# Three of sixteen sequences of a shared expert moved into the head of the next stage, and scatters that read their places directly

## Chip, core and metric

The kernel runs on one core of one Trainium2 chip. The metric is the device time of one execution in microseconds; lower is better. It is the median of several executions.

## What is computed

Four layers follow each other on 16 sequences of 256 tokens with 256 features, all in float32. Each is added to its input behind a layer norm, of which the second layer, a mixture of experts with a shared expert for all tokens, and the third, a state space layer, matter here.

```python
def _swiglu(t, wa, wb, wo):
    h = jax.nn.silu(t @ wa.T) * (t @ wb.T)
    return h @ wo.T
# layer 0, feed forward: 16 experts of width 176, top 2; shared width 352
scores = jax.nn.softmax(t @ gate_w.T, axis=-1)
weights, indices = jax.lax.top_k(scores, TOP_K)
for e in range(N_EXPERTS):
    w_e = jnp.sum(jnp.where(indices == e, weights, 0.0), axis=-1)
    y = y + _swiglu(t, w1[e], w3[e], w2[e]) * w_e[:, None]
z = _swiglu(t, sw1, sw3, sw2)          # the shared expert, of every token
return y + z
...
x = x + _layernorm(_L0_attn_ref(_layernorm(x), ...))
x = x + _layernorm(_L0_ffn_ref(_layernorm(x), ...))
x = x + _layernorm(_L1_attn_ref(_layernorm(x), ...))   # state space layer
x = x + _layernorm(_L1_ffn_ref(_layernorm(x), ...))    # 16 experts, top 8
```

## The kernel before

Each engine has a program of its own, written in the order in which it runs; semaphores tie them together. No scheduler moves anything: what a generator of steps yields first comes first on every engine that has a part in it. A step names its work, and each engine's function for that stage picks its share. x stays in SBUF (32 tiles of 128 tokens, two for a sequence).

The kernel goes through three parts. The first is attention, to about 436 us. The second is `SparseMoe`, the first mixture of experts. The third is `Tail`, the fused loop of the state space layer and the second mixture of experts, from about 822 us.

`SparseMoe` has two stages. In the **shared stage** `shared_steps` yields, for each of 16 sequences, the steps of the shared expert: "norm" (VectorE writes the normed rows), "turn_x" (TensorE transposes them in 4 pieces, ScalarE copies them out of PSUM), three chunks "up" (8 multiplications each, then silu on ScalarE and the product with the other half on VectorE, L769), and "down" (12 multiplications, L559; ScalarE copies the result, SyncE stores it to `results`). The hidden width of 704 makes three chunks for silu and product, of 128, 128 and 96 rows. The down step of a sequence stands behind the first up chunk of the next. Among these steps stand the "choose" steps (VectorE finds the two experts of each token and its place in a list sorted by expert) and, from the fifth sequence on, one "scatter" behind each chunk, for the 32 tiles. In a scatter VectorE writes a tile's rows into one of two buffers `pairs` (L685, L779), after it has waited for the DMAs that last read that buffer; GpSimd copies the places (L818), does an addition that nobody reads (L819), and issues two indirect DMAs (L822), which write the rows to `sorted_in` in HBM. SyncE waits for all scatters before it fetches the first sorted rows (L863).

In the **routed stage** 80 blocks of 128 sorted rows are fetched and go through their experts (L528, L599, L610, L620).

In the **tail**, `Tail.head` yields the steps with which the loop begins. "c_fetch" loads the three results of each token of a sequence, "c_sum" and "c_norm" (L2074 to L2089) add them and write the new x; "norm", "turn_x" (L1689), "feat" (L1701), "bcdt" (L1708), "turn_dt" (L1714), "dt", "table", "turn_dA" (L1731), "gate" (L1723), "conv" and "silu" prepare the state space layer of sequence 0; "turn_c" (L1740) and "xdt" (L1933) end this. Then `period` yields 18 rows of steps for each sequence, a table `THEN` saying what stands in which. The first scan of the decays (L1942, L1945) and its weighting (L1951) open period 0. Table loads of ScalarE (ACT_TABLE_LOAD) come where the activation function changes its set.

In PSUM there are eight banks; in the tail banks 4 to 6 (`UP_BANK`) and 7 (`SUM_BANK`) belong to the second mixture of experts and are unused in the head.

## Time and profile before

| | |
|---|---|
| median of 3 runs | 1965.39 us (1960.80 to 1970.16) |
| the profiled execution, its own time | 1962.86 us |
| span of its profile | 1961.1 us |
| busy share of the span | TensorE 93%, VectorE 64%, ScalarE 39%, GpSimd 22% |
| mean granted clock of TensorE | 0.96 of full |
| chain that ended last, by engine | TensorE 45%, issue 38%, VectorE 9%, GpSimd 4% |
| shared stage | 436 to 587 us |
| routed stage | 587 to 820 us |
| head of the tail, to the first scan weighting | 822 to 871 us |

A timeline row reads: start in us, duration in us, engine, line, operation, what is written and from what, shapes, how many instructions are merged. In brackets stands the idle time of the engine before it and what ended that. PE is TensorE's multiplications, PEld its weight loads, DVE VectorE, ACT ScalarE, POOL GpSimd, SPq the DMA queue of SyncE. A row of windows reads: stretch, its length, busy time (and instructions) of PE, PEld, DVE, ACT and POOL, the granted clock as a share of 2.4 GHz, the DMA engines' busy share, GB/s. Busy shares tell little here, since the stages have different bounds; the waits in each stage are what counts.

### The profile page before, as it was taken

How to read it: one execution, taken by the hardware profiler on the slowest of the kernel's cores; microseconds unless marked ns; L12 is line 12 of the kernel's file. 1: busy time of each engine (PE TensorE's matmuls, PEld its weight loads, DVE VectorE, ACT ScalarE, POOL GpSimd, SP SyncE). 2: the span in 40 equal slices, each digit the busy share in tenths (PEclk: the TensorE clock that was granted, in tenths of full speed). 3: DMA queues.
4: the chain of work that ended last, by engine and by line, in shares of the span. 5: the costliest groups of instructions: out<-in, count | busy, mean ns of one | idle time of the engine just before them, and what ended most of it. 6: DMA issues, size and time to landing. Idle time of an engine off the chain costs nothing.

```text
span 1961.1 us, 33597 instructions
## 1 busy us (share of the span) xinstructions
PE 1831.5 (93%) x9969; PEld 1414.6 (72%) x9987; DVE 1264.7 (64%) x3621; ACT 763.2 (39%) x1479; POOL 422.5 (22%) x708
## 2 busy tenths in 40 slices
PE   5999999979989999667999999999999999999998
PEld 3566666547776666445888888888888888888886
DVE  3677677527432222368778877887787778777843
ACT  1466666543223333234433343334333333433321
POOL 1244334331763444300100110011001100110000
PEclk9899999879998999867999999999999999999999
DMA  9900000001332333252012202220222022112210
GB/s 359 220 6 1 0 0 1 1 1 38 114 108 84 94 94 93 81 199 81 25 63 87 82 16 76 87 81 6 87 85 63 25 86 81 46 46 71 66 49 11
DMA packets 92119, 137.87 MB, mean 70 GB/s; under 512 B 18548, under 2 KB 76148, under 8 KB 91508
## 3 DMA queue, kind: packets, MB, share of 16 engines
q1 hardware_dynamic: 85108, 117.83, 19.0%
q0 software_dynamic: 6912, 18.92, 2.7%
q8 instruction: 38, 0.62, 0.1%
q14 instruction: 61, 0.50, 0.1%
HBM read 98.51 MB, written 38.22 MB: 70 GB/s over the span
## 4 chain that ended last, share of the span: by engine, by line
PE 45%; issue 38%; DVE 9%; POOL 4%; ACT 2%; DMA 1%; another core or an unknown queue 1%; DVEq 0%; SPq 0%; POOLq 0%; ACTq 0%
PE bank L599 6%; PE bank L184 5%; PE bank L1151 4%; PE bank L620 4%; PE bank L1216 3%; PE bank L1109 2%; PE bank L548 2%; PE bank L193 2%; PE bank L1157 2%; PE bank L1244 2%; PE bank L1139 2%; PE bank L559 1%; PE bank L610 1%; PE bank L1202 1%; PE bank L528 1%
## 5 line engine op out<-in xcount | busy, mean ns | idle before, releaser
L184 PE MATMUL bank<-moe_xT,up_w 128*128 128x256 f32 x2304 | 546.1, 380 | 0.0
L184 PEld LDWEIGHTS bank<-moe_xT,up_w 128*128 128x128 f32 x2304 | 438.7, 191 | 60.0
L227 ACT ACTIVATE moe_silu<-bank 128x256 f32<-128x256 f32 x288 | 110.4, 383 | 575.6 <-PE bank L184 572.4
L193 PE MATMUL bank<-down_w,moe_hT 128*128 128x256 f32 x1152 | 304.0, 387 | 3.5 <-ACT moe_y L230 2.1
L193 PEld LDWEIGHTS bank<-down_w,moe_hT 128*128 128x128 f32 x1152 | 207.1, 190 | 37.0 <-issue 6.4
L1390 DVE TENSOR_REDUCE q_slots<-bank 128x4 f32<-128x1024 f32 (+1 forms) x96 | 117.7, 1226 | 82.2 <-PE bank L1151 81.6
L1298 ACT ACTIVATE probs<-bank 128x1024 f32<-128x1024 f32 x96 | 98.1, 1022 | 100.4 <-PE bank L1157 100.4
L599 PE MATMUL bank<-up_w,moe_xT 128*128 x320 | 116.8, 488 | 0.7 <-ACT moe_xT L663 0.6
L794 DVE TENSOR_TENSOR moe_h<-moe_silu,bank 128x176 f32<-128x176 f32 x80 | 27.0, 338 | 138.8 <-issue 86.4
L1151 PE MATMUL bank<-kT,qT 16*128 16x256 f32 (+1 forms) x1024 | 115.3, 353 | 0.2 <-issue 0.2
L294 DVE TENSOR_TENSOR moe_hT<-moe_silu,bank 128x256 f32<-128x256 f32 x256 | 107.7, 421 | 8.8
L1157 PE MATMUL bank<-qmT,kT 17*128 17x512 f32 x384 | 111.2, 652 | 1.3 <-ACT probs L1298 1.3
L293 DVE TENSOR_TENSOR moe_silu<-moe_silu,up_w 128x256 f32<-128x256 f32 x192 | 81.1, 423 | 46.5 <-ACT moe_silu L227 41.0
L326 POOL TENSOR_TENSOR moe_prstd<-moe_pmv,minus_half 128x2 f32<-128x2 f32 x16 | 12.2, 759 | 451.7 <-DVE moe_pmv L304 451.7
L1151 PEld LDWEIGHTS bank<-kT,qT 16*128 16x128 f32 x1024 | 79.5, 193 | 31.5 <-issue 28.5
L548 PE MATMUL bank<-moe_s_xT,up_w 128*128 128x256 f32 (+1 forms) x384 | 90.5, 385 | 4.8 <-ACT moe_s_xT L638 2.5
L620 PE MATMUL bank<-down_w,moe_hT 88*128 x320 | 84.7, 387 | 3.8 <-issue 3.2
L838 POOL DMA_INDIRECT results<-moe_result,moe_home x80 | 79.2, 990 | 20.2 <-POOL pool_spare L837 15.0
L1945 DVE TENSOR_TENSOR_SCAN m<-m,delta 128x256 f32<-128x256 f32 x128 | 81.5, 678 | 2.2
L548 PEld LDWEIGHTS bank<-moe_s_xT,up_w 128*128 128x128 f32 (+1 forms) x384 | 69.4, 184 | 18.5 <-ACT moe_s_xT L638 3.3
L1923 DVE SCALAR_TENSOR_TENSOR conv<-feat,taps,conv 128x256 f32<-128x256 f32 x192 | 80.1, 478 | 1.8 <-ACT conv_bc L1839 1.2
L599 PEld LDWEIGHTS bank<-up_w,moe_xT 128*128 128x128 f32 x320 | 55.2, 192 | 28.5 <-issue 9.3
(287 smaller groups left out, 3181.5 us busy)
## 6 DMA issues: line engine op xcount, KB each, us to landing
up_w<-comb_rows SPq DMA_DIRECT2D x32, 768.0 KB, 6.0
m<-decay_rows SPq DMA_DIRECT2D x16, 1024.0 KB, 4.9
comb_got<-results SPq DMA_DIRECT2D x16, 768.0 KB, 7.7
moe_rows<-sorted_in SPq DMA_DIRECT2D x80, 128.5 KB
sorted_in<-zero SPq DMA_DIRECT2D x10, 1024.0 KB, 9.5
down_w<-comb_rows SPq DMA_DIRECT2D x16, 512.0 KB, 8.4
up_w<-in_up SPq DMA_DIRECT2D x2, 3168.0 KB, 15.0
up_w<-in_up SPq DMA_DIRECT2D x2, 2304.0 KB, 11.9
```

The costliest lines, as they stand in the source:

```text
L184: last = mm(k.bank[:, UP_BANK + i % 3, half * S:(half + 1) * S], m.w_up[:, c, at + half * m.inter:at + (half + 1) * m.inter], m.xT[:, par, ...
L193: last = mm(k.bank[:, SUM_BANK, j * D:(j + 1) * D], m.hT[:, i % 3, j * P:(j + 1) * P], m.w_down[:, m.expert(i), :], start=(i == 0 and j == ...
L227: nc.scalar.activation(m.silu[:, i % 3, :], k.bank[:, UP_BANK + i % 3, 0:S], ACT.Silu).then_inc(m.silu_ready, 1)
L294: tt(m.hT[:, i % 3, :], m.silu[:, i % 3, :], u, ALU.mult).then_inc(m.h_ready, 1)
L548: last = nc.tensor.matmul(k.bank[0:w, 2 + c, half * S:(half + 1) * S], m.w_up[:, f, lo + half * 2 * inter:lo + half * 2 * inter + w], m.s_ ...
L599: last = nc.tensor.matmul(k.bank[:, 2 + par, 0:2 * inter], m.xT[:, par, c, :], cols(m.w_up[:, c, :], expert, 2 * inter), start=(c == 0), s ...
L620: last = nc.tensor.matmul(k.bank[:, 6 + par, 0:D], m.hT[0:m.half, par, c, :], w_down[0:m.half, bass.ds(expert * 2 * D + c * D, D)], start= ...
L1151: last = mm(k.bank[:, SCORE_BANK + lane, r * keys:(r + 1) * keys], m.qT[rows, its, qb, half * per + r, :], m.kT[rows, its, 0:keys], start= ...
L1157: last = mm(k.bank[:, PROB_BANK + lane, :], m.kT[rows, par, phalf * P:(phalf + 1) * P], m.qmT[rows, pqb].rearrange("p r n -> p (r n)"), st ...
L1298: activation(m.probs[:, (i + 2 * par) % 4].rearrange("p g r n -> p (g r n)"), k.bank[:, PROB_BANK:PROB_BANK + PAIR, :].rearrange("p b n -> ...
L1390: v.tensor_reduce(m.q[:, par, qb, half * per:(half + 1) * per, heads[0]:heads[0] + PAIR, HD].rearrange("p r g -> p g r"), k.bank[:, SCORE_ ...
L1945: last = v.tensor_tensor_scan(to[:, 0:S], to[:, 0:S], m.delta[:], 0.0, ALU.mult, ALU.add)
```

## The change

Two things change in the shared stage. It runs over 13 sequences (`EARLY`) instead of 16. The 32 scatters are spread over the 27 places behind the chunks of sequences 4 to 12; five places hold two. GpSimd reads a tile's places directly from `places`, without the copy and the addition. There are two buffers of rows (`PAIR_ROWS`), as before.

The last three sequences, a, b and c in `head`, are computed in the head of the tail by new steps: l_norm, l_turn, l_up (three), l_h (three), l_down and l_end. They use the buffers and PSUM banks of the second mixture of experts, single buffers except for xT. Their stores go through SyncE's queue, and l_end, behind period 0, waits for them.

```diff
+PAIR_ROWS = 2
+EARLY = 13
...
+    places = chunks * (EARLY - SCATTERS_FROM)
...
-    for t in range(B):
+    for t in range(EARLY):
...
-            if t >= SCATTERS_FROM and tile < TILES:
+            place = chunks * (t - SCATTERS_FROM) + c + 1
+            while place > 0 and tile < -(-TILES * place // places):
                 yield "scatter", tile, 0
                 tile += 1
...
-        self.place = sb("moe0_place", [P, 4], U32)
-        self.pairs = sb("moe0_pairs", [P, 2, 2, ROW])
+        self.pairs = sb("moe0_pairs", [P, PAIR_ROWS, 2, ROW])
...
-            par = t % 2
-            if begun(t - 1):
-                dve.wait_ge(m.scattered[par], (t - par) * 16)
+            row = t % PAIR_ROWS
+            if t >= PAIR_ROWS:
+                dve.wait_ge(m.scattered[row], 2 * 16 * (t // PAIR_ROWS))
             for j in range(2):
-                normalise(m.pairs[:, par, j, 0:D], t)
-            v.tensor_copy(m.pairs[:, par, :, D].bitcast(U32), cols(k.pair_no, t, 2)).then_inc(m.rows_ready, 1)
+                normalise(m.pairs[:, row, j, 0:D], t)
+            v.tensor_copy(m.pairs[:, row, :, D].bitcast(U32), cols(k.pair_no, t, 2)).then_inc(m.rows_ready, 1)
...
-            par = t % 2
+            row = t % PAIR_ROWS
             pool.wait_ge(m.rows_ready, t + 1)
-            chain.link(g.tensor_copy(m.place[:, 2 * par:2 * par + 2], cols(m.places, t, 2)))
-            g.tensor_tensor(k.pool_spare[:, 0:1], k.minus_half[:, 0:1], k.minus_half[:, 0:1], ALU.add)
             for j in range(2):
-                at = bass.IndirectOffsetOnAxis(m.place[:, 2 * par + j:2 * par + j + 1], 0)
-                g.indirect_dma_start(m.sorted_in, at, m.pairs[:, par, j, :], None).then_inc(m.scattered[par], 16)
+                at = bass.IndirectOffsetOnAxis(m.places[:, 2 * t + j:2 * t + j + 1], 0)
+                g.indirect_dma_start(m.sorted_in, at, m.pairs[:, row, j, :], None).then_inc(m.scattered[row], 16)
...
+    def step(what, t, par, c):
+        n = t - EARLY
+        if what == "l_turn":
+            pe.wait_ge(s.xn_ready, t + 1)
+            pe.wait_ge(s.y_read, t)
+            for f in range(KD):
+                for j in range(SEQ_TILES):
+                    last = nc.tensor.transpose(k.bank[:, SUM_BANK, (f * SEQ_TILES + j) * P:(f * SEQ_TILES + j + 1) * P],
+                                               moe.xn[:, j, f * P:(f + 1) * P], k.ident[:])
+            last.then_inc(s.xT_full, 1)
+        if what == "l_up":
+            w, lo = s.wide(c), E * 2 * s.inter + c * P
+            pe.wait_ge(s.xT_ready, m.turns + n + 1)
+            if n > 0:
+                pe.wait_ge(s.h_ready, m.up(t - 1, c) + 1)
+            for half in range(2):
+                for f in range(KD):
+                    last = nc.tensor.matmul(k.bank[0:w, UP_BANK + c, half * S:(half + 1) * S],
+                                            s.w_up[:, f, lo + half * 2 * s.inter:lo + half * 2 * s.inter + w],
+                                            moe.xT[:, t % 2, f, :], start=(f == 0), stop=(f == KD - 1))
+            last.then_inc(s.up_full, 1)
+        if what == "l_down":
+            pe.wait_ge(s.h_ready, m.up(t + 1, 0))
+            for j in range(SEQ_TILES):
+                for c in range(s.shared_chunks):
+                    w = s.wide(c)
+                    last = nc.tensor.matmul(k.bank[:, SUM_BANK, j * D:(j + 1) * D], moe.hT[0:w, c, j * P:(j + 1) * P],
+                                            s.w_down[0:w, 2 * E + c, :], start=(c == 0), stop=(c == s.shared_chunks - 1))
+            last.then_inc(s.y_full, 1)
+        if what == "l_end":
+            pe.wait_ge(s.y_read, B)
...
+        n = t - EARLY
+        if what == "l_turn":
+            act.wait_ge(s.xT_full, m.turns + n + 1)
+            nc.scalar.copy(moe.xT[:, t % 2].rearrange("p c t -> p (c t)"), k.bank[:, SUM_BANK, :]).then_inc(s.xT_ready, 1)
+        if what == "l_up":
+            w = s.wide(c)
+            act.wait_ge(s.up_full, m.up(t, c) + 1)
+            if n > 0:
+                act.wait_ge(s.h_ready, m.up(t - 1, c) + 1)
+            nc.scalar.activation(moe.silu[0:w, c, :], k.bank[0:w, UP_BANK + c, 0:S], ACT.Silu).then_inc(s.silu_ready, 1)
+        if what == "l_down":
+            act.wait_ge(s.y_full, m.turns + n + 1)
+            if n > 0:
+                act.wait_ge(s.stored[(t - 1) % 2], 16 * ((t - 1) // 2 + 1))
+            nc.scalar.copy(moe.y[:].rearrange("p j d -> p (j d)"), k.bank[:, SUM_BANK, :]).then_inc(s.y_read, 1)
+        if what == "l_end":
+            for stored in s.stored:
+                act.wait_ge(stored, 16 * B // 2)
...
+        n = t - EARLY
+        if what == "l_norm":
+            if n > 0:
+                dve.wait_ge(s.xT_full, m.turns + n)
+            for j in range(SEQ_TILES):
+                last = normalised(k, moe.xn[:, j, :], SEQ_TILES * t + j)
+            last.then_inc(s.xn_ready, 1)
+        if what == "l_h":
+            w = s.wide(c)
+            dve.wait_ge(s.silu_ready, m.up(t, c) + 1)
+            if n > 0:
+                dve.wait_ge(s.y_full, m.turns + n)
+            k.nc.vector.tensor_tensor(moe.hT[0:w, c, :], moe.silu[0:w, c, :], k.bank[0:w, UP_BANK + c, S:2 * S],
+                                      ALU.mult).then_inc(s.h_ready, 1)
...
+        if what == "l_down":
+            sp.wait_ge(s.y_read, t + 1)
+            sp.dma_start(s.shared_rows(t), moe.y[:]).then_inc(s.stored[t % 2], 16)
+        if what == "l_end":
+            for stored in s.stored:
+                sp.wait_ge(stored, 16 * B // 2)
...
-        for what, t, i in (("c_fetch", 0, 0), ("c_sum", 0, 0), ("c_sum", 0, 1), ("c_norm", 0, 0), ("c_fetch", 1, 0),
-                           ("experts", 0, 0)):
+        a, b, c = range(EARLY, B)
+        yield "c_fetch", 0, 0, 0
+        for what, t, i in (("l_norm", a, 0), ("l_turn", a, 0), ("l_up", a, 0), ("c_sum", 0, 0), ("l_up", a, 1), ("c_sum", 0, 1),
+                           ("l_up", a, 2), ("l_h", a, 0), ("c_norm", 0, 0), ("l_h", a, 1), ("c_fetch", 1, 0),
+                           ("experts", 0, 0), ("norm", 0, 0), ("l_h", a, 2), ("l_norm", b, 0), ("norm", 0, 1),
+                           ("l_down", a, 0), ("turn_x", 0, 0), ("l_turn", b, 0), ("feat", 0, 0), ("l_up", b, 0), ("feat", 0, 1),
+                           ("l_h", b, 0), ("l_up", b, 1), ("bcdt", 0, 0), ("l_h", b, 1), ("l_up", b, 2), ("turn_dt", 0, 0),
+                           ("dt", 0, 0), ("table", 0, 0), ("conv", 0, 0), ("one_plus", 0, 0), ("l_h", b, 2), ("table", 0, 1),
+                           ("dt", 0, 1), ("conv", 0, 1), ("l_norm", c, 0), ("dt", 0, 2), ("table", 0, 2), ("turn_dA", 0, 0), ("decay_out", 0, 0), ("decay_in", 0, 0), ("l_down", b, 0),
+                           ("gate", 0, 0), ("conv", 0, 2), ("l_turn", c, 0), ("gate", 0, 1), ("conv", 0, 3), ("l_up", c, 0),
+                           ("silu", 0, 0), ("l_up", c, 1), ("c_sum", 1, 0), ("l_h", c, 0), ("l_up", c, 2), ("c_sum", 1, 1),
+                           ("l_h", c, 1), ("c_norm", 1, 0), ("turn_c", 0, 0), ("turn_c", 0, 1), ("l_h", c, 2),
+                           ("norm", 1, 0), ("norm", 1, 1), ("turn_x", 1, 0), ("l_down", c, 0), ("xdt", 0, 0)):
             yield what, t, t % 2, i
-        for what, i in (("norm", 0), ("norm", 1), ("turn_x", 0), ("feat", 0), ("feat", 1), ("bcdt", 0), ("turn_dt", 0), ("dt", 0), ("table", 0),
-                        ("conv", 0), ("one_plus", 0), ("table", 1), ("dt", 1), ("conv", 1), ("dt", 2), ("table", 2),
-                        ("turn_dA", 0), ("decay_out", 0), ("gate", 0), ("conv", 2), ("decay_in", 0), ("gate", 1), ("conv", 3), ("silu", 0)):
-            yield what, 0, 0, i
-        for what, i in (("c_sum", 0), ("c_sum", 1), ("c_norm", 0)):
-            yield what, 1, 1, i
-        for i in (0, 1):
-            yield "turn_c", 0, 0, i
-        for what, i in (("norm", 0), ("norm", 1), ("turn_x", 0)):
-            yield what, 1, 1, i
-        yield "xdt", 0, 0, 0
-        for t in (0, 1):
-            yield from self.period(t, t % 2)
+        yield from self.period(0, 0)
+        yield "l_end", B, 0, 0
+        yield from self.period(1, 1)
```

Places behind the chunks: on VectorE, before, in the fifth sequence of the shared stage (moe_pairs are the rows to scatter, moe_s_hT is the product of a chunk):

```order
466 L685 TENSOR_SCALAR moe_pairs<-x,next_norm 128x256 x2
467 L779 COPY moe_pairs<-pair_no 128x2
468 L769 TENSOR_TENSOR moe_s_hT<-moe_s_silu,bank 128x256
469 L685 TENSOR_SCALAR moe_pairs<-x,next_norm 128x256 x2
470 L779 COPY moe_pairs<-pair_no 128x2
471 L769 TENSOR_TENSOR moe_s_hT<-moe_s_silu,bank 96x256
```

and now:

```order
466 L689 TENSOR_SCALAR moe_pairs<-x,next_norm 128x256 x2
467 L792 COPY moe_pairs<-pair_no 128x2
468 L689 TENSOR_SCALAR moe_pairs<-x,next_norm 128x256 x2
469 L792 COPY moe_pairs<-pair_no 128x2
470 L782 TENSOR_TENSOR moe_s_hT<-moe_s_silu,bank 128x256
471 L689 TENSOR_SCALAR moe_pairs<-x,next_norm 128x256 x2
472 L792 COPY moe_pairs<-pair_no 128x2
473 L782 TENSOR_TENSOR moe_s_hT<-moe_s_silu,bank 96x256
```

The second pair of tiles stands ahead of the first product of the sequence; the rows of a third follow where the second was.

TensorE, from its first instruction in the head of the tail (L1689 transposes the normed rows of sequence 0), before:

```order
768 L1689 MATMUL bank<-ident,ssm_xn 128x128 x4
769 L1701 MATMUL bank<-ssm_xT,w_x 128x256 x8
770 L1708 MATMUL bank<-ssm_xT,w_bc 72x256 x2
771 L1714 MATMUL bank<-ident,feat_bc 128x72 x2
772 L1731 MATMUL bank<-ident,s_decay 8x128 x2
```

and now (L907, L917 and L926 are l_turn, l_up and l_down; L1813 is what L1689 was, L1825 the old L1701, L1832 the old L1708):

```order
753 L907 MATMUL bank<-ident,moe_xn 128x128 x4
754 L917 MATMUL bank<-moe_xT,up_w 128x256 x8
755 L917 MATMUL bank<-moe_xT,up_w 96x256 x4
756 L926 MATMUL bank<-down_w,moe_hT 128x256 x6
757 L1813 MATMUL bank<-ident,ssm_xn 128x128 x4
758 L907 MATMUL bank<-ident,moe_xn 128x128 x4
759 L1825 MATMUL bank<-ssm_xT,w_x 128x256 x4
760 L917 MATMUL bank<-moe_xT,up_w 128x256 x4
761 L1825 MATMUL bank<-ssm_xT,w_x 128x256 x4
762 L917 MATMUL bank<-moe_xT,up_w 128x256 x4
763 L1832 MATMUL bank<-ssm_xT,w_bc 72x256 x2
764 L917 MATMUL bank<-moe_xT,up_w 96x256 x4
```

One late sequence stands ahead of the transposes of sequence 0, and the chunks of the next stand between the parts of its projection.

VectorE at the same place, from the end of its set-up (neg_a), before:

```order
617 L2002 TENSOR_SCALAR neg_a<-pos_a 128x8
618 L2074 SCALAR_TENSOR_TENSOR comb_got<-comb_got,moe_weight 128x256 x2
619 L2075 BN_STATS comb_stat<-comb_got 128x6
620 L2074 SCALAR_TENSOR_TENSOR comb_got<-comb_got,moe_weight 128x256 x2
621 L2075 BN_STATS comb_stat<-comb_got 128x6
622 L45 MEMSET spare 128x1
623 L2079 BN_AGGR comb_mv<-comb_stat 128x2 x2
624 L2081 TENSOR_SCALAR comb_mv<-comb_mv 128x2
625 L2086 TENSOR_SCALAR comb_got<-comb_got,comb_mv,comb_rstd 128x256 x2
626 L2089 TENSOR_TENSOR x<-x,comb_got 128x512
```

and now (L977 is the product of a late chunk, L689 writes the rows of a late sequence):

```order
606 L2126 TENSOR_SCALAR neg_a<-pos_a 128x8
607 L689 TENSOR_SCALAR moe_xn<-x,next_norm 128x256 x2
608 L2198 SCALAR_TENSOR_TENSOR comb_got<-comb_got,moe_weight 128x256 x2
609 L2199 BN_STATS comb_stat<-comb_got 128x6
610 L2198 SCALAR_TENSOR_TENSOR comb_got<-comb_got,moe_weight 128x256 x2
611 L2199 BN_STATS comb_stat<-comb_got 128x6
612 L45 MEMSET spare 128x1
613 L2203 BN_AGGR comb_mv<-comb_stat 128x2 x2
614 L2205 TENSOR_SCALAR comb_mv<-comb_mv 128x2
615 L977 TENSOR_TENSOR moe_hT<-moe_silu,bank 128x256
616 L2210 TENSOR_SCALAR comb_got<-comb_got,comb_mv,comb_rstd 128x256 x2
617 L2213 TENSOR_TENSOR x<-x,comb_got 128x512
```

The rows of the first late sequence are written first, and its first product stands between the statistics of sequence 0 and their use.

## Rows read from the trace of the kernel before

**Rows 1.** The shared stage in stretches of 9 us, all engines (one of them).

```profile
501.00:510.00 9.00, 8.16 (x40) 6.72 (x39) 4.36 (x14) 2.29 (x5) 7.15 (x13) 1.00 0.34 118
```

**Rows 2.** Timeline of GpSimd: first scatter, one whole tile, the last issue.

```profile
482.86 0.18 POOL L818 COPY moe_place<-moe_places 128x2 uint32<-128x2 uint32 x1 [52.08 <-DVE moe_pairs L779]
...
489.16 0.18 POOL L818 COPY moe_place<-moe_places 128x2 uint32<-128x2 uint32 x1
489.43 0.19 POOL L819 TENSOR_TENSOR pool_spare<-minus_half 128x1 f32<-128x1 f32 x1
489.77 0.99 POOL L822 DMA_INDIRECT sorted_in<-moe_pairs,moe_place  x1 [0.15 <-issue]
491.07 0.97 POOL L822 DMA_INDIRECT sorted_in<-moe_pairs,moe_place  x1 [0.30 <-issue]
...
577.89 0.97 POOL L822 DMA_INDIRECT sorted_in<-moe_pairs,moe_place  x1 [0.30 <-issue]
```

**Rows 3.** Timeline of VectorE: the rows of one pair of tiles.

```profile
493.87 0.74 DVE L685 TENSOR_SCALAR moe_pairs<-x,next_norm 128x256 f32<-128x256 f32 x2 [1.35 <-DMA sorted_in<-moe_pairs,moe_place]
494.52 0.16 DVE L779 COPY moe_pairs<-pair_no 128x2 uint32<-128x2 uint32 x1
```

**Rows 4.** Timeline of TensorE: down steps (L559), and the first routed block.

```profile
484.58 2.76 PE L559 MATMUL bank<-down_w,moe_s_hT 128*128 128x256 f32 x12
...
567.83 2.76 PE L559 MATMUL bank<-down_w,moe_s_hT 128*128 128x256 f32 x12
...
576.05 2.76 PE L559 MATMUL bank<-down_w,moe_s_hT 128*128 128x256 f32 x12
...
583.18 2.86 PE L559 MATMUL bank<-down_w,moe_s_hT 128*128 128x256 f32 x12 [0.92 <-DVE moe_s_hT L769]
589.65 0.66 PE L528 MATMUL bank<-ident,moe_rows 128*128 128x128 f32 x2 [3.61 <-DMA moe_rows<-sorted_in]
```

**Rows 5.** Timeline of SyncE's queue: the first fetch of the routed blocks.

```profile
587.17 0.90 SPq L863 DMA_DIRECT2D moe_rows<-sorted_in  x2
```

**Rows 6.** Timeline of TensorE in the head of the fused loop.

```profile
817.76 1.12 PE L620 MATMUL bank<-down_w,moe_hT 88*128 x4 [0.56 <-ACT moe_hT L673]
835.66 1.09 PE L1689 MATMUL bank<-ident,ssm_xn 128*128 128x128 f32 x4 [16.77 <-DVE ssm_xn L1888]
...
853.21 0.59 PE L1731 MATMUL bank<-ident,s_decay 128*8 128x128 f32 x2 [6.64 <-ACT s_decay L1820]
...
868.46 1.22 PE L1758 MATMUL bank<-cT,bT 16*128 16x256 f32 x2
```

**Rows 7.** Timeline of ScalarE and VectorE in that head.

```profile
824.14 1.28 ACT L1791 ACT_TABLE_LOAD   x1 [6.53 <-DVE a_lim L2000]
...
858.39 1.01 DVE L2074 SCALAR_TENSOR_TENSOR comb_got<-comb_got,moe_weight 128x256 f32<-128x256 f32 x2
...
864.69 0.73 DVE L1888 TENSOR_SCALAR ssm_xn<-x,ssm_mv,ssm_rstd 128x256 f32<-128x256 f32 x2 [0.80 <-POOL ssm_rstd L2020]
...
867.33 1.29 DVE L1933 TENSOR_TENSOR xdt<-down_w,s_dt 128x512 f32<-128x512 f32 x2 [1.91 <-ACT down_w L1853]
...
870.68 0.95 DVE L1951 TENSOR_TENSOR m<-m,bank 128x768 f32<-128x768 f32 x1
```

**Rows 8.** The head in stretches of 2 us, with TensorE's granted clock.

```profile
840.00:842.00 2.00, 1.23 (x4) 0.45 (x3) 0.00 (x0) 0.59 (x1) 0.00 (x0) 0.66 0.97 415
...
860.00:862.00 2.00, 1.67 (x4) 0.77 (x3) 1.13 (x6) 0.29 (x1) 0.69 (x1) 0.54 0.00 0
```

**Rows 9.** Timeline at the start of the shared stage: one sequence.

```profile
438.70 5.34 PE L548 MATMUL bank<-moe_s_xT,up_w 128*128 128x256 f32 x16 [0.73 <-ACT moe_s_xT L638]
442.35 0.38 ACT L644 ACTIVATE moe_s_silu<-bank 128x256 f32<-128x256 f32 x1 [2.40 <-PE bank L548]
442.77 0.42 DVE L769 TENSOR_TENSOR moe_s_hT<-moe_s_silu,bank 128x256 f32<-128x256 f32 x1 [6.03 <-ACT moe_s_silu L644]
...
447.41 0.58 ACT L638 COPY moe_s_xT<-bank 128x512 f32<-128x512 f32 x1
```

## What I predicted, before any run

> **What bounds the kernel now.** I read three places, each with the view that shows its end: the shared stage, the hand-over to the routed blocks, and the head of the fused loop.
>
> In the shared stage, first the windows. While scatters run, GpSimd is busy 7.15 of 9 us and TensorE is no longer full, 8.16 of 9 [rows 1]. The timeline of GpSimd says why. A tile is a copy of its two places, a spare addition and two indirect DMAs: 0.99, a gap of 0.30, and 0.97, then the next tile [rows 2]. From 482.86 to the end of the last issue at 578.86 there are 32 tiles, 3.00 us each. VectorE fills the rows of tile n+2 only when tile n has landed: the second issue of the tile at 489.77 ends at 492.04, and the next rows are begun at 493.87, 1.83 later; writing them takes 0.81 to 494.68 [rows 3]. VectorE works in order, so the products that TensorE needs for its down step stand behind that wait. Without a wait a sequence takes TensorE 8.22 us (567.83 to 576.05); over the ten sequences from 484.58 to 576.05 it took 9.15 [rows 4]. So the scatters set the pace from the fifth sequence on. The stage ends with the sixteenth down step at 586.04, and the first fetch of sorted rows is issued at 587.17 [rows 4, 5].
>
> In the head, TensorE is idle 16.77 us until 835.66 and again 6.64 us until 853.21, from 846.57 [rows 6]; the first scan weights (L1951) start at 870.68 [rows 7]. That is where the change puts the work it takes from the shared stage. The idle time looks like free room, but most of the steps ahead of 870.68 form one chain through VectorE and ScalarE, and these engines work in order too.
>
> **Part 1: three sequences fewer in the shared stage.** It now ends with the last scatter, not with TensorE, because 32 tiles must pass in nine sequences, where there were twelve. On GpSimd copy and addition go; a tile is 0.99 + 0.30 + 0.97 and a gap that the trace doesn't show: 0.15 (behind the addition) to 0.30 (between two issues) [rows 2]. I take 0.30, the case without an instruction between: 2.56. The two buffers make a second limit: 2.26 of issues and a gap of 0.30, 1.83 to land, 0.81 to write, 0.07 to be noticed is 5.27 for two tiles, 2.63 each [rows 2, 3]. It is the larger one. A sequence with three tiles needs 7.9 and is held by TensorE's 8.22; one with four needs 10.5. The rounding of 32 tiles over 27 places puts four into five sequences and three into four: 5 x 10.5 + 4 x 8.2 = 85.3. From 482.9 this gives 568.2, then 1.8 to land and a few tenths for the queue (the fetch came 0.5 after the copy of the last result before): a first fetch at 571 instead of 587.17, **16 us earlier**. The ends: with 2.43 per tile (the gap of 0.15 and a faster landing) sequences take 9.7 and 8.2, 81.4, a fetch at 567, -20. At the old pace of 3.00 the last issue ends at 579 as before, a fetch at 581, -6. The last down step is done before either, so it hides.
>
> The landing can be put against a page. The row shows 2.80 us from the start of an issue (491.07) to the next rows. The Trainium skill, "DMA: Bandwidth & Descriptors", in its anatomy of the GpSimd path, fits 2.0 us plus bytes over 436 GB/s, 2.3 for these 132 KB; by that estimate the issues alone would bind, 84 instead of 85.3, and the gain would be 17.
>
> **Part 2: the same three sequences in the head.** One is 24 up multiplications, 12 down and 4 transposes, 8.2 us at the full clock (above) and 16.4 at half; 24.7 and 49 for three. I lay the new order out on the old clock times of the head, up to L1951.
>
> - Start: the late rows are written behind neg_a, 825.9 to 826.6 (0.74, as in [rows 3]). TensorE resumes near 826.8 instead of 835.66, after 8 us of idling and so at half clock: in the first row of [rows 9] 16 multiplications take 5.34, half of them at 1.2 GHz. In both heads seen the full clock came 3.5 us into dense work [rows 8, 9]. So: transposes 1.1, copy 0.6 [rows 9], the first chunk 3.5 at half, two chunks 1.8 each, and the last late product at 837.7 (silu 0.38 and product 0.42 behind it [rows 9]).
> - VectorE does the first c_norm and norm between these products, and norms the second late sequence first: xn of sequence 0 is written at 839.2, where it had been written before the transposes of 835.66. TensorE then does down 2.8 (as in [rows 4]), turn 0.6, turn 0.6, 0.2 of waits for copies, four parts of the inner projection and up (7.0), then bcdt, a third up, turn_dt (3.0). This lasts from 837.8 to 852.0 instead of ending at 846.57 [rows 6]: **+5.4**.
> - From turn_dt to the decay transpose it took 6.64 [rows 6]. Into this chain come: a silu that stands ahead of the exponential and its table load, 0.4 and 1.28 [rows 7]; part of this is made up while VectorE waits, but it also gets one product and two norms (0.4 and 0.7). I count 8.6: decay transpose at 860.6, **+7.4** in all.
> - TensorE has idled 8.6 and is at half clock. Down 5.2, one gate 2.9, then at the full clock (after 8 us, as it took from 853.21 to about 861.8 [rows 8]) turn, copy, second gate, first up chunk: the product of the last late sequence can start at 873.7. VectorE, which had summed the second sequence at once before, waits for it. Behind stand the rest of c_sum, c_norm and norm, 7.0 from 858.39 to 865.42 before, and xdt 1.3 [rows 7], with 0.8 for the two other late products, half of it in the wait for GpSimd: 874.1 + 7.0 + 0.4 + 1.3, xdt ends at 882.8 against 868.62. TensorE has the transposes of sequence 1 (0.6) and the last down (2.8) behind norm, from 881.5, and 0.9 for the matrix that the weights need: L1951 at 885.8 against 870.68, **+15**.
>
> What follows is bound by VectorE and shifts with it. The ends: +12 if the clock rises earlier; +25 if it stays at half behind 860.6 (13 us of full-speed work left there).
>
> The table loads can be put against a page. The rows show 1.28 for a load, with the next activation at once behind it (the load at 824.14 ends at 825.42). The Trainium skill, "ScalarE: Activation LUTs", on what ACT_TABLE_LOAD costs, counts a drain of 1.38 too, 2.66 for each switch. By that one switch on the chain costs 1.4 more, and the loss would be 16.
>
> The stores of the three late results add three DMAs to SyncE's queue, the second and third ahead of the fetch for sequence 2. That fetch waited for c_norm of sequence 1 before; it still does, and has the whole first period to land, so I count nothing. Line l_end waits for stores issued one period earlier: nothing.
>
> **Sum.** The profiled execution took 1962.86. 1962.9 - 16 + 15 = 1961.9. The median of the three runs is 2.5 above this execution, so I forecast **1964** for the median.
>
> **Rivals.**
>
> *Cold TensorE (slower).* Denser scatters stop TensorE longer: in a four-tile sequence it idles 10.5 - 8.2 = 2.3 us in one piece. A gap of 0.92 leaves the clock up; one of 3.61 drops it (0.66 for two transposes behind it, half speed) [rows 4]. If 2.3 is enough, three-tile sequences lose up to 3 us each. The same in the head, where every hand-over can keep it at 1.2 GHz: +25 instead of +15. It decides when the granted clock behind 860 is still 0.5 at 870. Then 1974 to 1979; I take 1976. The Trainium skill, "TensorE: Matmul & The Clock Gate", says half rate is the default and activity releases it; dense work in the head should then raise it.
>
> *The work is hidden (faster).* TensorE's two idle stretches in the head sum to 23.4 us [rows 6], nearly the 24.7 that is added. If VectorE's waits for late products fall where it had nothing to do, the head grows by 5 or 6 only. For it: VectorE waits too before 835. Against: the layout above, in which VectorE stands waiting for late products with its own work queued behind. 1964 - 9 = 1955, and with the shorter tile 1951.
>
> *The scatter doesn't get shorter (the change does not do what it says there).* If the pace stays 3.00 per tile because the wait for landing grows as the issues close up, removing two small instructions from GpSimd gains nothing: Then -6 and +15 on the median of 1965, 1974.
>
> **Chances.** Forecast case, parts nearly cancel: 0.48. Cold TensorE 0.22, hidden 0.15, scatter not shorter 0.15. About 0.5%, 9.8 us, is what a measurement of this kernel can tell from no change, so the borders are 1955.6 and 1975.2. The forecast case lies within (a twentieth on either side outside); of the hidden case four fifths is faster; of the cold case most is slower; the scatter case is four fifths the same. Faster 0.16, same 0.60, slower 0.24. The range 1952 to 1979 takes in the bounds of both parts but not their joint ends.
>
> **What would show it.** Distances are safe from the shift of part 1; I take them from the last down of the routed blocks (817.76 before). Right: the first fetch near 571, GpSimd's tiles 2.6 apart, the decay transpose 43 us behind that down instead of 35.5, L1951 68 behind it instead of 52.9. Wrong: a distance to L1951 under 60 or over 75, tiles at 2.9 us, or a granted clock of 0.5 while the scatters run. If both parts hold and the time still differs, something outside these two stretches moved, for which the order of instructions gives no reason.

## The result, and the profile after

| | before | after |
|---|---|---|
| median of 20 runs each | 1964.84 us (1960.8 to 1972.26) | 1973.01 us (1964.63 to 1977.54) |
| profiled execution: its time, its span | 1962.86, 1961.1 | 1969.38, 1967.6 |
| granted TensorE clock | 0.962 | 0.964 |
| ratio of the medians' runs | | 1.0046, 95% interval 1.0033 to 1.0059 |

The changed kernel is slower by 0.46%, 8 us, and the interval of the ratio lies wholly above 1; I had forecast 1964, a hair faster than before. The range (1952 to 1979) holds the time, the direction is wrong.

**The shared stage.** Views of the profile after, each of a few rows: SyncE's queue with the first fetch of sorted rows (L870 is the old L863, [rows 5]); then GpSimd's issues; one of VectorE's rows; then ScalarE and TensorE. Columns are start, length, engine, line, operation, and in brackets the idle time before and what ended it.

```profile
580.73 0.83 SPq L870 DMA_DIRECT2D moe_rows<-sorted_in  x2
...
502.08 0.96 POOL L832 DMA_INDIRECT sorted_in<-moe_pairs,moe_places  x1 [2.59 <-DVE moe_pairs L792]
503.34 0.98 POOL L832 DMA_INDIRECT sorted_in<-moe_pairs,moe_places  x1 [0.30 <-issue]
...
508.42 0.96 POOL L832 DMA_INDIRECT sorted_in<-moe_pairs,moe_places  x1 [0.30 <-issue]
...
516.62 0.96 POOL L832 DMA_INDIRECT sorted_in<-moe_pairs,moe_places  x1 [0.30 <-issue]
521.03 0.96 POOL L832 DMA_INDIRECT sorted_in<-moe_pairs,moe_places  x1 [3.45 <-DVE moe_pairs L792]
```
```profile
511.03 0.74 DVE L689 TENSOR_SCALAR moe_pairs<-x,next_norm 128x256 f32<-128x256 f32 x2 [1.16 <-DMA sorted_in<-moe_pairs,moe_places]
```

The first fetch comes at 580.73 instead of 587.17: 6.4 earlier, not 16. The issues themselves are as short as I took them, 1.26 apart, 2.53 for a tile. But GpSimd stands still in between (2.59, 3.45, and four more waits of 1.8 to 2.0), and so 32 tiles take 95 us, 2.98 each (the gap of 0.30 behind the last issue counted). The landings are not the cause: the second issue of a tile ends at 509.38 and VectorE begins the next rows at 511.03, 1.65 later, where it had been 1.83 [rows 2, 3]. In the long waits of GpSimd VectorE's pair rows come late; and VectorE is late because it waits for ScalarE:

```profile
510.56 0.38 ACT L652 ACTIVATE moe_s_silu<-bank 128x256 f32<-128x256 f32 x1 [2.26 <-PE bank L556]
517.72 0.58 ACT L657 COPY moe_s_y<-bank 128x512 f32<-128x512 f32 x1 [6.77 <-remote]
519.19 0.38 ACT L652 ACTIVATE moe_s_silu<-bank 128x256 f32<-128x256 f32 x1 [0.89 <-remote]
519.47 0.58 ACT L646 COPY moe_s_xT<-bank 128x512 f32<-128x512 f32 x1
```

and TensorE in the same stretch:

```profile
512.62 1.89 PE L556 MATMUL bank<-moe_s_xT,up_w 128*128 128x256 f32 x8
514.35 0.60 PE L546 MATMUL bank<-ident,moe_s_xn 128*128 128x128 f32 x4
514.78 1.89 PE L556 MATMUL bank<-moe_s_xT,up_w 128*96 128x256 f32 x8
520.11 3.38 PE L556 MATMUL bank<-moe_s_xT,up_w 128*128 128x256 f32 x8 [3.43 <-ACT moe_s_xT L646]
```

The down step had ended by 512.8 (the next multiplications start at 512.62), the transposes at 515. ScalarE copied the first only at 517.72 and the second at 519.47. Of its 6.77 us of idling the first 1.8 are a wait for the down step; in the other 4.9 nothing that the profile shows held it. TensorE ran out of work for 3.43, and its clock fell: eight multiplications took 3.38 instead of 1.89. This view has no counterpart in my prediction, in which ScalarE was always on time.

**The head** went nearly as laid out. TensorE after the last routed down step (compare [rows 6, 7]; L1855 is the old L1731, L1813 the old L1689), and the first scan weights on VectorE (L2075, the old L1951):

```profile
810.63 1.13 PE L628 MATMUL bank<-down_w,moe_hT 88*128 x4 [0.56 <-ACT moe_hT L681]
819.74 1.08 PE L907 MATMUL bank<-ident,moe_xn 128*128 128x128 f32 x4 [7.98 <-DVE moe_xn L689]
...
831.95 0.60 PE L1813 MATMUL bank<-ident,ssm_xn 128*128 128x128 f32 x4
...
851.61 0.59 PE L1855 MATMUL bank<-ident,s_decay 128*8 128x128 f32 x2 [8.45 <-ACT s_decay L1944]
...
870.71 0.66 PE L1813 MATMUL bank<-ident,ssm_xn 128*128 128x128 f32 x4 [2.85 <-DVE ssm_xn L2012]
871.20 4.43 PE L926 MATMUL bank<-down_w,moe_hT 128*128 128x256 f32 x12
...
906.58 1.12 PE L1864 MATMUL bank<-ident,conv 128*128 128x128 f32 x4 [6.57 <-ACT conv L1972]
```
```profile
876.51 0.95 DVE L2075 TENSOR_TENSOR m<-m,bank 128x768 f32<-128x768 f32 x1 [2.70 <-PE bank L1883]
```

The decay transpose is 40.98 behind the last routed down (35.45 before), L2075 65.9 behind it (52.9 before).

For the experiments I use one marker further on, the transposes of conv that end TensorE's wait of 6.57, and measure from where TensorE goes idle behind the last routed down (start of the first step of the head minus its idle time). Before, the marker was this row:

```profile
898.49 1.12 PE L1740 MATMUL bank<-ident,conv 128*128 128x128 f32 x4 [6.57 <-ACT conv L1848]
```

so 898.49 - (835.66 - 16.77) = **79.6** ([rows 6] for the second term), and after 906.58 - (819.74 - 7.98) = **94.8**. The two executions then differ so: first scatter +0.15 (483.91 against 483.76, the first issue behind the copy of 482.86 in [rows 2]), stage from there to the first fetch 96.8 against 103.4, -6.6; routed blocks -0.7; head +15.2; the rest -1.6. Sum +6.5, the difference of the spans.

### The profile page after: what moved, and what is told of

It is laid out like the page before. It is cut to its first block, busy times and chain, and to the rows that moved or that the text cites. A ratio compares the mean times of both kernels' runs of the same rounds, so it can differ in the third digit from the quotient of the medians.

```text
span 1967.6 us, 33536 instructions
## 1 busy us (share of the span) xinstructions
PE 1835.6 (93%) x9986; PEld 1416.1 (72%) x9987; DVE 1265.4 (64%) x3621; ACT 765.2 (39%) x1481; POOL 407.9 (21%) x644
## 4 chain that ended last, share of the span: by engine, by line
PE 45%; issue 38%; DVE 9%; POOL 4%; ACT 2%; DMA 1%; another core or an unknown queue 1%; DVEq 0%; SPq 0%; POOLq 0%; ACTq 0%
PE bank L607 5%; PE bank L184 5%; PE bank L1275 4%; PE bank L628 4%; PE bank L1340 3%; PE bank L1233 2%; PE bank L193 2%; PE bank L1281 2%; PE bank L1263 2%; PE bank L1368 2%; PE bank L556 1%; PE bank L618 1%; PE bank L1326 1%; PE bank L536 1%; PE bank L1243 1%
## 5 line engine op out<-in xcount | busy, mean ns | idle before, releaser
L556 PE MATMUL bank<-moe_s_xT,up_w 128*128 128x256 f32 (+1 forms) x312 | 76.0, 393 | 10.4 <-ACT moe_s_xT L646 9.2
L832 POOL DMA_INDIRECT sorted_in<-moe_pairs,moe_places x64 | 61.8, 966 | 86.0 <-DVE moe_pairs L792 68.3
```

The source lines that it names most:

```text
L556: last = nc.tensor.matmul(k.bank[0:w, 2 + c, half * S:(half + 1) * S], m.w_up[:, f, lo + half * 2 * inter:lo + half * 2 * inter + w], m.s_ ...
```

## Experiments

Two numbers are read from each trace: the **stage**, from the first scatter to the first fetch (103.4 before, 96.8 after), and the **head**, as just defined. The runs fell on three chips; I call them A (e1 to e4, e17, e18), B (e5 to e12) and C (e13 to e16). The kernel before ran beside each group: 1964.3, 1964.2, 1963.8, 1964.0 and 1965.2. It makes no difference between the chips. The four kernels that ran on A and on B do, as it turned out. On which chip the kernels were measured for the result above is not recorded. Stage and head come from one trace for each run.

| label | what | chip | median us | ratio to before, 95% | stage | head |
|---|---|---|---|---|---|---|
| e1 | no late work | A | 1944.7 | 0.990 (0.988, 0.992) | 86.3 | 79.2 |
| e2 | 16 sequences, direct places | A | 1957.4 | 0.996 (0.995, 0.998) | 97.7 | 79.3 |
| e3 | changed, old issue | A | 1971.0 | 1.003 (1.002, 1.005) | 97.3 | 92.7 |
| e4 | changed, four rows | A | 1959.1 | 0.997 (0.995, 0.999) | 84.3 | 92.4 |
| e5 | changed | B | 1975.6 | 1.005 (1.004, 1.007) | 96.1 | 92.6 |
| e6 | changed, zero rows | B | 1972.9 | 1.004 (1.002, 1.005) | 97.6 | 92.5 |
| e7 | one late, four rows | B | 1962.9 | 0.999 (0.998, 1.000) | 99.4 | 79.5 |
| e8 | two late, four rows | B | 1967.8 | 1.002 (1.001, 1.003) | 102.0 | 85.0 |
| e9 | changed | B | 1972.9 | 1.004 (1.002, 1.005) | 97.5 | 95.6 |
| e10 | no late work | B | 1956.2 | 0.995 (0.993, 0.997) | 98.6 | 79.7 |
| e11 | changed, four rows | B | 1976.8 | 1.005 (1.004, 1.007) | 102.4 | 92.6 |
| e12 | 16 sequences, direct places | B | 1966.3 | 1.000 (0.999, 1.002) | 107.5 | 79.3 |
| e13 | changed, eight bytes | C | 1977.7 | 1.007 (1.004, 1.009) | 102.4 | 92.8 |
| e14 | changed, old issue | C | 1972.4 | 1.004 (1.002, 1.005) | 96.9 | 95.8 |
| e15 | one late | C | 1948.4 | 0.992 (0.990, 0.993) | 90.1 | 79.3 |
| e16 | one late, old issue | C | 1960.2 | 0.998 (0.996, 0.999) | 95.3 | 79.2 |
| e17 | changed | A | 1963.5 | 1.000 (0.998, 1.001) | 87.4 | 95.4 |
| e18 | one late | A | 1949.9 | 0.992 (0.991, 0.994) | 88.4 | 79.3 |

### First group: the parts apart (chip A)

**e1_no_late.** The head of before and no late steps; the shared expert of the last three sequences is left out:

```diff
-        a, b, c = range(EARLY, B)
-        yield "c_fetch", 0, 0, 0
-        for what, t, i in (("l_norm", a, 0), ("l_turn", a, 0), ...
+        for what, t, i in (("c_fetch", 0, 0), ("c_sum", 0, 0), ("c_sum", 0, 1), ("c_norm", 0, 0), ...
```

> The shared stage of the changed kernel (13 sequences), the head of before; the shared expert of the last three sequences is left out (their result rows are filled with zeros early in the program). It splits the change in two. Reading of the two traces: the shared stage gained 6.4 us (first fetch 580.7 instead of 587.2) and the head lost 15. Then this kernel takes 1965 - 6 = 1959 and the late work costs 1973 - 1959 = 14. Rival: part of the loss came from elsewhere (the routed blocks, the loop behind the head); then this kernel is above 1961 with a first fetch still near 581.

Measured 1944.7 and a stage of 86.3, while the stage's code is that of the changed kernel, which had taken 96.8. Both theories missed: the time is 28 below the changed kernel, not 14.

**e2_direct16.** `EARLY = 16` and the head of before.

> Only the direct places and the new rule for the scatters: all 16 sequences in the shared stage, head of before, 32 tiles over 36 places. Theory A (the issues of GpSimd set the pace in the kernel before, 3.00 per tile): a tile of 2.6 makes three of them 7.9, under TensorE's 8.22, so ten sequences get 0.93 us shorter, the first fetch comes at 578 and the time is 1956. Theory B (VectorE's waits for its pair rows and the products queued behind them set the pace whatever an issue costs): tiles stay near 3.0, first fetch 584 or later, 1962 or more.

1957.4, stage 97.7 (from 103.4): theory A. The direct places alone are worth 7 us of the median on this chip.

**e3_old_issue.** On GpSimd, in the changed kernel:

```diff
+            chain.link(g.tensor_copy(m.place[:, 2 * row:2 * row + 2], cols(m.places, t, 2)))
+            g.tensor_tensor(k.pool_spare[:, 0:1], k.minus_half[:, 0:1], k.minus_half[:, 0:1], ALU.add)
             for j in range(2):
-                at = bass.IndirectOffsetOnAxis(m.places[:, 2 * t + j:2 * t + j + 1], 0)
+                at = bass.IndirectOffsetOnAxis(m.place[:, 2 * row + j:2 * row + j + 1], 0)
```

> The changed kernel with the copy of the places and the spare addition back ahead of each pair of scatters on GpSimd; everything else as changed. Theory A (in the changed kernel GpSimd's issues no longer bind, VectorE's pair rows do, GpSimd waits 1.8 to 3.5 us for them every few tiles): the two small instructions fall into those waits, 1973 to 1976. Theory B (each tile's length still counts, the waits come on top): 32 tiles by 0.4 us, 13 us more, a first fetch near 594 and 1986.

1971.0, which looks like theory A. It isn't: beside e1 on the same chip the stage went from 86.3 to 97.3, 11 us or 0.34 per tile. The reference of my expectation, a stage of 96.8 for direct places, did not hold on this chip.

**e4_four_rows.** `PAIR_ROWS = 4`.

> The changed kernel with four pairs of rows instead of two; nothing else is changed. Theory A (VectorE waits for a landing with the products for the down step queued behind, that stops TensorE and then silu, and so the next rows come late): four buffers take the wait away, tiles come 2.53 apart, GpSimd binds, first fetch 484 + 32 x 2.53 + 5 = 570 to 573 instead of 580.7, TensorE's gaps over 3 us go, time 1973 - 9 = 1964. Theory B (ScalarE's stalls that end with no releaser, up to 8.3 us, hold silu and the copies back, whatever rows there are): first fetch 579 or later, 1971 or more.

Stage 84.3, first fetch 570.36, 1959.1: the fetch that theory A said, and a time 5 below the one it said. But e1 with two rows was at 86.3, so four rows can't be what gained the other 10. (The 8.3 us in the expectation is a misreading of the trace after: that wait of ScalarE, until 493.70, ends 0.04 us behind the down step, which had itself begun late.)

### Second group: is it the kernel? (chip B)

**e5_again**, the changed kernel unaltered, and **e6_zero_rows**, which has the one thing that e1 had added:

```diff
-    pool.wait_ge(m.zeroed, 2 * 16 * ZERO_FILLS)
+    pool.wait_ge(m.zeroed, 2 * 16 * ZERO_FILLS + 16 * (B - EARLY))
...
+            for t in range(EARLY, B):
+                sp.dma_start(first.shared_rows(t), k.zero[:].unsqueeze(1).to_broadcast([P, SEQ_TILES, D])).then_inc(first.zeroed, 16)
```

> The changed kernel once more, unaltered, for a second trace beside the other runs. Its shared stage took 96.8 us from the first scatter to the first fetch, with gaps of up to 4.5 us in front of silu and products; the same instructions in the kernel without late work took 86.3, tiles 2.65 apart, as my forecast had them. Theory A (the gaps belong to this kernel in most executions): stage 93 to 97 again, median 1973. Theory B (the gaps are a matter of the single execution): this trace shows about 86, and the distance of 28 us between the medians of the two kernels must lie elsewhere, in the head.

> The changed kernel with the three early transfers that the kernel without late work had (zeros into the result rows of the last three sequences, written over later). If these transfers, or the place of what follows them, are what made its shared stage 10 us shorter: stage 86 and 1963. If the late work in the program is what makes the shared stage longer, or nothing does in particular: as the changed kernel, 1973.

Stages of 96.1 and 97.6: the long stage comes back each time, and the zero rows have nothing to do with it.

**e7_one_late_four_rows** and **e8_two_late_four_rows**: four rows, `EARLY = 15` and 14, and in the head the steps of missing sequences are skipped (the edit of e7; in e8 it is `a, b, c = EARLY, EARLY + 1, B`):

```diff
-        a, b, c = range(EARLY, B)
+        a, b, c = EARLY, B, B
...
-            yield what, t, t % 2, i
+            if t < B or what not in LATE_STEPS:
+                yield what, t, t % 2, i
```

> Direct places, four pairs of rows, and only the last sequence in the head (15 in the shared stage, 32 tiles over 33 places). Stage: 16 sequences with direct places took 97.7 from first scatter to fetch; one fewer is 8.2 less, 89.5, if TensorE binds and nothing stalls. Head: 3 to 4 more than before, from the place of the transposes of sequence 0 in the two traces (3.4). Against the kernel with direct places alone (1957) that is -8 + 4 = 1953. Rival: the late sequence costs as much as its share of the whole, 5 of 15 at least, and the stage keeps stalls: 1957 or more.

> The same with the last two sequences in the head (14 in the shared stage, 32 tiles over 30 places). Stage: ten sequences of 8.2 or 32 tiles of 2.59, whichever is longer, 84.5. Head: the decay transposes 5.5 later, as in the changed kernel, but no third product ahead of the norms of sequence 1 and no third down step; +6 to +8 of its 13 to 15. Against four rows with three late sequences (1959) that is 1952. Rival: the head's loss is the time of VectorE and ScalarE for each late sequence alike, 10 of 15, and nothing is won: 1955 or more.

Both were slower than expected, by 10 and 16: the stage took 99.4 and 102.0 where 89.5 and 84.5 were counted, with four rows. The head was the other way about, **79.5 with one late sequence, as with none**, and 85.0 with two.

### Third group: the same four kernels on one chip (B again)

> The changed kernel, unaltered, on one chip beside the three that follow. So far its shared stage took 96 to 98 us in three traces, and 86.3 in the one trace of the same stage without late work; but those were taken on different chips. Theory A (it is the kernel): here too the stage takes 96 to 98 and the time is 28 above that of the kernel without late work. Theory B (it is the chip: on some chips ScalarE and the landings stall while scatters run): changed kernel and kernel without late work show the same stage here, 86 or 97 both, and differ by the head alone, 13 to 15.

> The kernel without late work again (the shared expert of the last three sequences is left out). Theory A (the kernel): stage 86, 1945. Theory B (the chip): the stage as that of the changed kernel beside it, and 13 to 15 less than its time.

> The changed kernel with four pairs of rows again. On the first chip its stage took 84.3 and it gave 1959. Theory A (four rows mend the stage, whatever the chip): 1959 and 84 to 86. Theory B (ScalarE stalls while scatters run on this chip, as in the two kernels with fewer late sequences and four rows, stage 99 and 102): stage 95 or more and 1970.

> Direct places alone again, 16 sequences in the shared stage. Theory A (pace of TensorE, whatever the chip): stage 97.7, 1957. Theory B (ScalarE stalls on this chip while scatters run): the stage 102 to 106 and 1962 to 1966.

Theory B each time. Without late work the stage is 98.6 where it was 86.3 on chip A; four rows give 102.4 instead of 84.3, direct places alone 107.5 instead of 97.7. The medians moved by 11.5, 17.7 and 8.9. On one chip the changed kernel and the one without late work differ by 17, of which the head is 15.9 (95.6 - 79.7). Four rows give the shortest stage of the three-late kernels on A and the longest on B. A was measured ahead of B and again after it (e17, e18), and looked the same both times.

What differs is ScalarE. For every silu and copy of ScalarE from the first scatter on I take the distance from the end of what it needs (TensorE's multiplications, VectorE's product where the buffer must be free, its own instruction before) to its start. In the ten traces from A and C this is never more than 0.04 us. In each of the eight from B, 8 to 14 of these instructions start more than 0.5 late, the worst by 2.6 (e12) to 7.95 (e7). The trace after has 13, the worst 4.9, and the trace of before has 11, the worst 2.55. VectorE's products and TensorE's steps are never more than 0.3 late in this sense in any trace, and the next pair rows come 1.8 to 1.9 behind the issues in e5, e9 and e17 alike (medians over the tiles for which VectorE stood waiting), so landings are not slower on B. Nor can a slow transfer hold ScalarE: of its instructions only the copy of a down step's result waits for one, and most of the late ones are silu and copies of transposes.

Kernel e11 on chip B, a row of TensorE, then ScalarE, then GpSimd:

```profile
495.62 1.89 PE L556 MATMUL bank<-moe_s_xT,up_w 128*128 128x256 f32 x8
```
```profile
497.35 0.58 ACT L657 COPY moe_s_y<-bank 128x512 f32<-128x512 f32 x1 [3.75 <-remote]
503.75 0.38 ACT L652 ACTIVATE moe_s_silu<-bank 128x256 f32<-128x256 f32 x1 [5.81 <-remote]
511.43 0.58 ACT L646 COPY moe_s_xT<-bank 128x512 f32<-128x512 f32 x1 [7.30 <-remote]
```
```profile
505.18 0.96 POOL L832 DMA_INDIRECT sorted_in<-moe_pairs,moe_places  x1 [0.30 <-issue]
...
508.97 0.96 POOL L832 DMA_INDIRECT sorted_in<-moe_pairs,moe_places  x1 [0.30 <-issue]
514.73 0.96 POOL L832 DMA_INDIRECT sorted_in<-moe_pairs,moe_places  x1 [4.80 <-DVE moe_pairs L792]
```

The multiplications for the silu of 503.75 ended at 497.5. GpSimd issued 20 scatters in one run from 483.54 to 509.93, from 487 on 1.26 apart. The silu of 503.75 fell into this run, 5.8 late. The copy of 511.43, 7.3 late, came 1.5 us after the issues stopped, which they did only because VectorE, waiting for ScalarE, no longer filled rows. The same kernel on chip A, with the same dense issues:

```profile
498.37 0.58 ACT L657 COPY moe_s_y<-bank 128x512 f32<-128x512 f32 x1 [2.21 <-PE bank L567]
500.09 0.38 ACT L652 ACTIVATE moe_s_silu<-bank 128x256 f32<-128x256 f32 x1 [1.14 <-PE bank L556]
501.50 0.59 ACT L646 COPY moe_s_xT<-bank 128x512 f32<-128x512 f32 x1 [1.02 <-PE bank L546]
```

Another mark goes with it. In the traces of chip B, and in those of the kernel before and of the first trace of the changed kernel, records of landings are missing, for the scatters and for the fetches of the routed stage: the profile's list of DMA issues has no time to landing. First e9 on chip B, then e17 on chip A, the same kernel:

```profile
sorted_in<-moe_pairs,moe_places POOLq DMA_INDIRECT x64
moe_rows<-sorted_in SPq DMA_DIRECT2D x80, 128.5 KB
```
```profile
sorted_in<-moe_pairs,moe_places POOLq DMA_INDIRECT x64, 2.8
moe_rows<-sorted_in SPq DMA_DIRECT2D x80, 128.5 KB, 2.1
```

So "remote" and "issue" in such a trace can mean a wait whose end was not recorded; that ScalarE was late is read from the ends of the TensorE steps, not from these words. In the routed stage of the same traces, where landings are missing too, none of ScalarE's copies and silu is more than 0.04 late (GpSimd issues one indirect DMA for each block there, 2.9 us apart).

### Fourth group: what of the scatters does it? (chip C)

**e13_eight_bytes** (all result rows are also filled with zeros early, not shown):

```diff
-                g.indirect_dma_start(m.sorted_in, at, m.pairs[:, row, j, :], None).then_inc(m.scattered[row], 16)
+                g.indirect_dma_start(m.small, at, m.pairs[:, row, j, 0:2], None).then_inc(m.scattered[row], 16)
```

> The changed kernel with scatters of 8 bytes per row instead of 1028, into a tensor of their own; the routed experts then work on rows of zeros and all result rows are filled with zeros early, so their part of the result is left out. The number of issues, their spacing and the number of rows stay. On the chips where ScalarE stalls while scatters run: Theory A (the issues themselves, close behind one another on GpSimd, hold ScalarE back): the stalls of 3 to 8 us stay, stage 95 or more. Theory B (the bytes that the scatters move do it): the stalls go, stage 84 to 87.

> The changed kernel with copy and spare addition back ahead of each pair of scatters. On the first chip, without stalls, this cost the stage 11 us against direct places (97.3 to 86.3). Theory A (on a chip where ScalarE stalls, the stalls come from unbroken issues; two small instructions per tile break them up): stage 96 to 98 here too, the same as direct places give on this chip, and 1971 to 1973. Theory B (stalls come whatever the spacing): both add up, stage 104 or more and 1980.

Neither told its theories apart, since chip C has no such stalls. Whether two small instructions for each tile break the stalls up, as e14 asked, has an answer all the same, in the trace of before: copy and addition stand between the pairs there, and ScalarE is late eleven times, by up to 2.55. Spacing of this kind does not prevent the stalls; whether it shortens them is open. e13 gave something else: the stage got *longer* with 8 bytes per row, 102.4. VectorE waited 49.3 us in 24 waits for landings; in e1, with 1028 bytes, 38.9 in 28. (The changed kernel itself did not run on C; its stage on A is 87.4, and where a kernel ran on both, the stages agree within 2.) First e13, then e1:

```profile
DVE moe_pairs L690 <- DMA small<-moe_pairs,moe_places: 49.3, 24, 5.2
```
```profile
DVE moe_pairs L689 <- DMA sorted_in<-moe_pairs,moe_places: 38.9, 28, 4.0
```

e14 repeats e3 (96.9 and 97.3): without stalls the old issue costs the stage 10 us. Its tiles are 2.98 apart in both, and 2.98 in the trace of before with its stalls: with the old issue the pace is the same with stalls and without, which fits the equal medians of the kernel before on all chips.

**e15_one_late**: as e7 with `PAIR_ROWS = 2`. **e16_one_late_old_issue**: the same with the two instructions of e3.

> Direct places, two pairs of rows, only the last sequence in the head. In the trace with four rows one late sequence cost the head nothing (79.5 us from the last down step of the routed blocks to the convolution transposes of period 1, as before; two cost 5.4, three 13 to 15). Stage 90 on a chip without stalls, 97 to 99 on one with them: 1950 or 1958. Rival: two rows stall VectorE as well, 102 or more, and 1962.

> The same with copy and spare addition on GpSimd as in the kernel before: only the number of sequences in the shared stage and the rule for the places differ from it. If spacing prevents ScalarE's stalls: 32 tiles of 3.0 and 3, stage 99, the head unchanged, 1964 - 5 = 1959 on any chip. If it doesn't: as before or above, 1964.

e15 is 1948.4, **0.8% faster than before**; stage 90.1, head 79.3. e16 is 1960.2, stage 95.3: one late sequence with the old issue is worth 4.

Why one late sequence costs the head nothing is seen on TensorE, e15 first and then before:

```profile
807.84 1.12 PE L628 MATMUL bank<-down_w,moe_hT 88*128 x4 [0.56 <-ACT moe_hT L681]
816.96 1.09 PE L907 MATMUL bank<-ident,moe_xn 128*128 128x128 f32 x4 [7.99 <-DVE moe_xn L689]
...
845.04 0.59 PE L1855 MATMUL bank<-ident,s_decay 128*8 128x128 f32 x2 [7.10 <-ACT s_decay L1944]
845.43 3.62 PE L1847 MATMUL bank<-ssm_xT,w_g 128*128 128x256 f32 x8
849.73 1.99 PE L1847 MATMUL bank<-ssm_xT,w_g 128*128 128x256 f32 x8 [0.69 <-ACT gate L1949]
854.22 0.66 PE L1864 MATMUL bank<-ident,conv 128*128 128x128 f32 x4 [2.49 <-ACT conv L1972]
```
```profile
857.89 3.78 PE L1723 MATMUL bank<-ssm_xT,w_g 128*128 128x256 f32 x8 [0.69 <-ACT gate L1825]
864.16 0.66 PE L1740 MATMUL bank<-ident,conv 128*128 128x128 f32 x4 [2.49 <-ACT conv L1848]
```

The decay transpose is 37.2 behind the last routed down, 1.8 later than before. But the second half of the gate now runs at the full clock, 1.99 instead of 3.78, and gives the 1.8 back: the transposes of conv start 46.4 behind, before and now.

### Fifth group: the changed kernel on a chip without stalls (A)

> The changed kernel, unaltered, once more beside the kernel with one late sequence. On a chip where ScalarE stalls between dense issues: stage 97, 1973, as before. On a chip without the stalls (as those of the first and of the fourth set of runs) the theory says what no run has shown yet: stage 86, and 12 less than on the other chips, 1960 to 1962.

> Direct places, two pairs of rows, only the last sequence in the head. On a chip without stalls: stage 90, 1948 as before. On a chip with them, if they cost it what they cost four rows and one late sequence there (stage 99): 1957 to 1960, still below the kernel before.

e17: **1963.5, ratio 1.000 (0.998, 1.001)**. The unaltered changed kernel is level with the kernel before on chip A and 0.4 to 0.5% slower on chip B. Its stage is 87.4; both are a little above what the expectation had for a chip without stalls (1960 to 1962, 86). e18 confirms e15 on a second chip. With one late sequence and two rows no run fell on chip B, so what it gives there is open; with four rows it was level there (e7).

Theory B of e9 is thus shown: the missing 10 us of the stage hang on the chip, and the late instructions of ScalarE are, besides the missing records, the only difference that I found in the traces of the stage. No run takes them away on chip B. What of the scatters holds ScalarE back there is **not settled**. For the density of the issues speaks that the six stalls of over 6 us (in e7, e8, e9 and e11) lie in unbroken runs of issues and end 1.2 to 2.2 us behind the last of a run, and that the routed stage has no stall. Against density alone speaks that 52 of the 113 late instructions in the ten traces with stalls start while an issue is under way, and that the trace of before has stalls. Bytes, the number of rows in flight and the recording itself (each timed run is recorded) are not excluded.

## Why the prediction was wrong, and where right

**Part 1, the two-buffer limit: 16 forecast, 6.4 in the trace after. This is the step that failed.** The step was "A sequence with three tiles needs 7.9 and is held by TensorE's 8.22; one with four needs 10.5", with every engine but these three prompt. On chip A this is what happens. I had 2.63 per tile; e17 shows 2.69 and e1 2.65. I had 571 - 483.8 = 87.2 for the stage; 87.4 and 86.3. With -16.0 in the stage and +15.8 in the head (to the marker) e17 took 1963.5, where I had forecast 1964. On chip B it is 2.95 to 3.00, and in the trace after 2.98; "tiles at 2.9 us" was my own sign of being wrong. The step failed there on an engine that it did not contain: ScalarE, off every path in my layout, was up to 4.9 us late in the trace after and up to 6.6 in e9, the stage lost 10 us by it, and +15 in the head was no longer balanced. The trace of before had signs of it. Its ScalarE is late eleven times in this stretch, and I took such waits for the slack of an idle engine. TensorE had ended the multiplications for this silu at 522.1, ScalarE its own last instruction at 522.8:

```profile
520.10 1.99 PE L548 MATMUL bank<-moe_s_xT,up_w 128*128 128x256 f32 x8 [0.39 <-issue]
```
```profile
525.32 0.38 ACT L644 ACTIVATE moe_s_silu<-bank 128x256 f32<-128x256 f32 x1 [2.55 <-remote]
```

**The rival that came out.** "The scatter doesn't get shorter" gave -6 and 1974; measured -6.4 and 1973. Its size fits by luck, its mechanism doesn't: landings did not take longer (1.65 behind the issue in the trace after, as read above, against 1.83), and on chip A the scatter did get shorter.

**Part 2, the head, +15: right as a mechanism, some 2 too large at its own place.** Measured +13.0 at L2075 (65.9 against 52.9), for which the forecast of +15 was made, and +15.2 at the marker further on. In ten traces with three late sequences the head is 92.4 to 92.8 six times and 94.8 to 95.8 four times. The split goes with TensorE's clock behind its idle time of 2.85. Two executions of the changed kernel, e5 and then e17:

```profile
866.10 0.66 PE L1813 MATMUL bank<-ident,ssm_xn 128*128 128x128 f32 x4 [2.86 <-DVE ssm_xn L2012]
866.59 2.76 PE L926 MATMUL bank<-down_w,moe_hT 128*128 128x256 f32 x12
```
```profile
855.23 1.11 PE L1813 MATMUL bank<-ident,ssm_xn 128*128 128x128 f32 x4 [2.85 <-DVE ssm_xn L2012]
856.13 4.80 PE L926 MATMUL bank<-down_w,moe_hT 128*128 128x256 f32 x12
```

The same gap, and once the full clock holds, once it is at half: 2.0 us for the twelve multiplications, and in all six of the lower heads the gap left the clock up. L2075 is +11.4 to +11.8 in these six and +13.0 to +16.3 in the other four, so 1.4 of the +13.0 are this fall of the clock, which I had not laid out. The decay transpose came 5.5 later where I had 7.4. The mis-sized term is "the last late product at 837.7": the pieces that I named in front of it (1.1, 0.6, 3.5, 3.6, 0.8 from 826.8) add up to 836.4. The down step began 18.6 behind the last routed down; 837.8 is 20.0. From it to the end of turn_dt I had 14.2, measured 13.9, and from there to the decay transpose 8.6 and 8.4.

**What the sum hid.** I priced the late work as one block of three. Its parts are not alike: 0 for the first (79.6 to 79.3), 5.5 for the second (85.0), 7 to 11 for the third. In part 1 it is the reverse. With direct places the stage is 97.7 with 16 sequences, 88 to 90 with 15 and 86 to 87 with 13: the first sequence taken out is worth 7.6 to 9.3, the next two together 1 to 4, since from then on the scatters end last. I had both facts in hand: TensorE idles 16.77 in one piece at the start of the head [rows 6], where one sequence of 8.2 at the full clock fits, and three tiles to a sequence take 7.9, less than its 8.22 on TensorE, so the first sequence taken out counts in full and only where four tiles come to a sequence do the scatters hold the others back.

**The other rivals.** *Cold TensorE* is partly so. Its sign in the head did not come: four transposes at 865.87 took 0.60, the full clock. In the stage a gap of 3.43 dropped the clock (the row at 520.11), one of 2.52 in e17 did not, and the 4.13 in front of the first down step behind the first scatters did (0.60 from 489 to 493). That gap I had not laid out: the rule puts two tiles at the first place, so VectorE waits 3.96 for a landing ahead of a product that TensorE needs. It stands in e1 and e17 too, and is in the 86 to 87. *The work is hidden* is true of one sequence in three.

**The pages.** By the totals the two estimates from the Trainium skill stay undecided: with "DMA: Bandwidth & Descriptors" I had 17 for part 1 and without it 16, and the stage was 16.0 shorter in e17 and 17.1 in e1 than in the one trace of before, which has the late ScalarE in it. The terms are decided. A scatter landed 2.7 (e1) to 2.8 us (e17) after its issue, where the fit of the Trainium skill, "DMA: Bandwidth & Descriptors", in its anatomy of the GpSimd path, gives an estimate of 2.3. The Trainium skill, "ScalarE: Activation LUTs", on what ACT_TABLE_LOAD costs, counts a drain of 1.38 at each table switch. The rows after show none, neither ahead of the load nor behind it. A load of 1.28 from 847.46, when the conv before it had just ended (846.85 + 0.58), is followed by its activation at 848.75.

```profile
847.46 1.28 ACT L1941 ACT_TABLE_LOAD   x1
848.75 0.22 ACT L1941 ACTIVATE s_ln<-s_w 128x16 f32<-128x16 f32 x1
```

## What to carry to other kernels

Price work that is moved in pieces, at both ends: the first piece often fits an idle stretch for nothing and the last piece is no longer what the place it leaves waits for, so the best amount lies between none and all (here one sequence of three: 0.8% faster instead of level or slower). A trace of one chip can hold waits that end with no releaser; before they are called slack, ask what happens if they grow with the change, and look at a second chip before a difference under 1% is explained by the code.

## What the runs showed that I had not expected

- The same program differs by chip in one stage: 87.4 (e17) and 96 to 98 us (e5, e9) for 32 tiles of scatters beside dense work, 12 us between the medians of e1 and e10, and 17.7 between those of e4 and e11, while the medians of the kernel before lie within 1.4.
- On chip B ScalarE starts instructions up to 8 us after their inputs are ready (7.95 in e7, 7.3 in e11) while GpSimd issues indirect DMAs; VectorE and TensorE do not. On A and C it is never more than 0.04.
- Scatters of 8 bytes per row are no faster than of 1028: median 3.1 us to landing (e13) against 2.8 (e17), and the stage was 15 us longer. Why is open.
- Two small instructions ahead of each pair of scatters cost 0.3 us per tile of the loop on a chip without stalls (2.98 in e3 and e14, against 2.65 in e1 and 2.69 in e17).
- TensorE's full clock survived an idle time of 2.52 us (e17), and of 2.85 in six of ten traces only.
